# A causal linear attention in another order and a 64-tap convolution with one product a channel

## The reference, cut to what matters

```python
def _feat(x):
    return jax.nn.elu(x) + 1.0
def step(carry, xs):
    Si, Zi = carry
    q, k, v = xs
    Si = Si + jnp.einsum('bhd,bhk->bhdk', k, v)
    Zi = Zi + k
    num = jnp.einsum('bhd,bhkd->bhk', q, Si)
    Vi = num / (q * Zi + EPS_CAUSAL)
    return ((Si, Zi), Vi)
...
Q_lin = _feat(Q)
K_lin = _feat(Kp)
V_lin = _causal_linear_attn(Q_lin, K_lin, V)
return new_values @ Wo + bo
```

```python
K = jnp.einsum('md,ldk,dk->lk', C, A_powers, B)
...
conv_full = jnp.fft.irfft(Uf * Kf[None], n=n, axis=1)
start = (L - 1) // 2
y = conv_full[:, start:start + seq_len, :]
y = y + D[None, None, :] * u
```

## Time and profile before

| | before |
|---|---|
| median of 3 runs | 3556.96 us |
| profiled execution | 3555.08 us |
| its span | 3553.3 us |
| mean granted clock of PE | 0.911 |
| PE busy over the span | 2896.8 us (82%) |
| DVE busy over the span | 2011.3 us (57%) |
| first cross attention, from its first key update to its end | 998.2 to 1197.3 us |
| convolution stage | 2310.8 to 2402.6 us |

### The profile page before, as it was taken

How to read it: one execution, slowest core, us unless ns; L and a number is a source line. 1 busy time by engine, 2 the same in 40 slices (tenths; PEclk the granted TensorE clock), 3 DMA queues, 4 the chain that set the end, 5 groups by cost and what they waited for, 6 DMA issues and landing times. The chain is left out here.

```text
span 3553.3 us, 59085 instructions
## 1 busy us (share of the span) xinstructions
PE 2896.8 (82%) x21229; PEld 2114.5 (60%) x21229; DVE 2011.3 (57%) x5009; ACT 1663.1 (47%) x3692; POOL 543.8 (15%) x530
## 2 busy tenths in 40 slices
PE   6999999999777788588799764556899969997897
PEld 5777777776555567356566531445696545554685
DVE  6776677767566623678666668626211673444323
ACT  6666666765432222366577527213332335554221
POOL 2111101110122142100000000000210003333422
PEclk8999999999988799799899887787899989999799
DMA  3111111110100268300000000051695010000486
GB/s 125 45 36 37 37 51 44 38 37 28 50 3 1 90 216 302 106 1 2 24 11 8 28 0 0 0 99 61 237 343 210 24 52 26 25 24 23 151 278 208
DMA packets 143184, 273.73 MB, mean 77 GB/s; under 512 B 50576, under 2 KB 105104, under 8 KB 138032
## 3 DMA queue, kind: packets, MB, share of 16 engines
q1 hardware_dynamic: 126544, 237.66, 20.7%
q0 software_dynamic: 8688, 23.78, 1.8%
q10 hardware_dynamic: 7664, 8.51, 0.7%
HBM read 222.17 MB, written 47.74 MB: 76 GB/s over the span
## 5 line engine op out<-in xcount | busy, mean ns | idle before, releaser
L3005 ACT ACTIVATE L0a_ex<-bank,L0a_nb 128x128 f32<-128x128 f32 x512 | 145.7, 368 | 124.9 <-PE bank L2934 124.4
L1430 POOL TENSOR_TENSOR L3x_p<-L3x_p,L3x_rsum 128x512 f32<-128x512 f32 x128 | 130.7, 1041 | 413.6 <-DVE L3x_rsum L1501 413.6
L3271 DVE TENSOR_TENSOR L0a_ru<-bank,L0a_um 128x512 f32<-128x512 f32 x128 | 88.2, 689 | 176.5 <-PE bank L2926 162.0
L1483 DVE CUSTOM_DVE_ANT_0 L3x_s<-bank,L3x_bias 128x512 f32<-128x512 f32 x128 | 87.1, 682 | 177.4 <-PE bank L1259 177.4
L3262 DVE SCALAR_TENSOR_TENSOR L0a_xf<-L0a_xc,L0a_conv,L0a_xf 128x256 f32<-128x256 f32 x432 | 178.3, 481 | 9.5 <-ACT L0a_xf L3067 8.0
L3183 POOL TENSOR_TENSOR L0a_sum_sq<-L0a_sum_sq,L0a_sq 128x512 f32<-128x512 f32 x56 | 73.1, 1306 | 697.1 <-ACT L0a_sq L3102 697.1
L2848 PE MATMUL bank<-x_feat,L0a_wx 128*128 128x256 f32 x576 | 138.2, 391 | 4.1 <-ACT L0a_xc L3054 4.1
L2934 PE MATMUL bank<-L0a_ru,L0a_vm 128*128 128x512 f32 x256 | 136.6, 616 | 0.0
L2891 PE MATMUL bank<-x_feat,L0a_wz 128*128 128x256 f32 x512 | 118.4, 382 | 8.5 <-DVE L0a_yacc L3362 6.2
L1483 DVE CUSTOM_DVE_ANT_0 L1x_s<-bank,L1x_bias 128x256 f32<-128x256 f32 x256 | 92.9, 420 | 56.3 <-PE bank L1259 41.1
L2848 PEld LDWEIGHTS bank<-x_feat,L0a_wx 128*128 128x128 f32 x576 | 108.7, 195 | 25.4 <-issue 7.0
(11 more groups left out here) (707 smaller groups left out, 7615.4 us busy)
## 6 DMA issues: line engine op xcount, KB each, us to landing
L2f_wt<-in_L2f_w SPq DMA_DIRECT2D x23, 2180.0 KB, 9.7
L0f_wt<-in_L0f_w SPq DMA_DIRECT2D x39, 898.0 KB, 6.4
L3f_wt<-in_L3f_w SPq DMA_DIRECT2D x39, 768.0 KB, 5.4
L0a_wx<-in_L0a_wx SPq DMA_DIRECT2D x72, 256.0 KB, 3.1
L0a_wz<-in_L0a_wz SPq DMA_DIRECT2D x32, 512.0 KB, 4.1
L2a_band<-conv_taps SPq DMA_DIRECT2D x4, 2048.0 KB, 21.3
context_keys_values<-L2f_zeros ACTq DMA_DIRECT2D x32, 256.0 KB, 4.3
L0f_xs<-rows_by_expert SPq DMA_DIRECT2D x39, 128.5 KB, 3.4
```

Source lines behind the costliest of these rows:

```text
L1430: nc.gpsimd.tensor_tensor(p_, p_, rsum[g // n % 2][:, g % n, :].to_broadcast([P, NK]), ALU.mult).then_inc(sig("divided"), 1)
L1483: ins = vec.tensor_tensor_reduce(out=s[:, at:at + nk], in0=bank[:, at:at + nk], in1=bias[r % 2][:, e, :], scale=-scale, scalar=3e38, op0=A ...
L3005: last = a(ex[g % 3][:, j, b * P:(b + 1) * P], bank[:, at:at + P], ACT.Exp, bias=nb[r % 2][:, b, h:h + 1])
L3271: rv.empty(vec.tensor_tensor(ru[g % 2][:], bank[:].rearrange("p (j t) -> p j t", j=2), um[:].unsqueeze(1).to_broadcast([P, 2, T]), ALU.mult))
```

## The change

In the first cross attention the query projection of the next row moves from step 2 to step 1, its value projection from step 3 to step 2. DVE's bias add of the row before moves from after masks and reciprocal of step 2 to ahead of the masks. The tap sums move from step 1, two rows late, to step 3, one row late, after the masks and before the key update.

In the convolution the reversed tokens are written as two halves of a window (first and second), and each channel is one product: 64 columns of taps, 32 columns of tokens (2 halves of 16 tiles), 64 partitions of a bank, even channels in the lower 64 and odd ones in the upper. One constant matrix takes the place of two. The copies are five for a row, six rows on ACT and two on DVE, from a bank of its own for each row. A full bank is added to x_res with four additions.

```diff
@@ layer2_attn
-        moved = sb("moved", [P, B, TB + 1, D])
+        window = sb("window", [P, 2, NT, D])
+        first, second = window[:, 0], window[:, 1]
...
+        BY_DVE = (3, 6)
+        def take(eng, copy, r):
+            eng.wait_ge(sig("flipped"), r + 1)
+            bank = c.banks[r][:].rearrange("p (t d) -> p t d", t=TB)
+            ts = slice(TB * r, TB * r + TB)
+            copy(first[0:96, ts, :], bank[0:96])
+            copy(first[96:128, TB * r + 1, :], bank[96:128, 0])
+            copy(second[64:128, ts, :], bank[0:64])
+            copy(second[32:64, ts, :], bank[96:128])
+            return copy(second[0:32, TB * r, :], bank[64:96, 1])
...
-                    xs = c.x[:, :, q * PER_BANK:(q + 1) * PER_BANK]
-                    vec.tensor_tensor(xs, xs, c.banks[q][:].rearrange("p (d t) -> p t d", t=NT), ALU.add)
+                    xs = c.x[:, :, q * PAIRS * 2:(q + 1) * PAIRS * 2].rearrange("p t (j e) -> p e t j", e=2)
+                    for e in range(2):
+                        for half in range(2):
+                            taken = c.banks[q][e * L:(e + 1) * L, :].rearrange("p (j h t) -> p h t j", h=2, t=NT)
+                            own = xs[half * L:(half + 1) * L, e]
+                            vec.tensor_tensor(own, taken[:, half], own, ALU.add)
...
-                    for kind in range(2):
-                        for i in range(2):
-                            last = nc.tensor.matmul(flip_bank(n, kind, i)[:], flip[:, kind, :],
-                                                    xn[n % 2][:, 2 * i:2 * i + 2, :].rearrange("p t d -> p (t d)"), start=True, stop=True)
+                    for i in range(2):
+                        nc.tensor.matmul(c.banks[2 * n + i][:], flip[:], xn[n % 2][:, 2 * i:2 * i + 2, :].rearrange("p t d -> p (t d)"),
+                                         start=True, stop=True).then_inc(sig("flipped"), 1)
...
-                    for q, (window, half) in enumerate(quarters):
-                        taps = band[g][:, j, half * L // 2:(half + 1) * L // 2]
-                        last = nc.tensor.matmul(c.banks[d // PER_BANK][q * L // 2:(q + 1) * L // 2, at:at + NT], taps, window(d),
-                                                start=True, stop=True)
+                    n, e = divmod(d, 2)
+                    at = n % PAIRS * 2 * NT
+                    last = nc.tensor.matmul(c.banks[n // PAIRS][e * L:(e + 1) * L, at:at + 2 * NT], band[g][:, j, :],
+                                            window[:, :, :, d], start=True, stop=True)
@@ layer0_xattn, tensor
-                        if gi == 2 and r + 1 < ROWS:
+                        if gi == 1 and r + 1 < ROWS:
                             pe.wait_ge(sig("sliced"), 2 * (r + 2))
                             features(r + 1, a_ring, wq, xb)
+                        if gi == 2 and r + 1 < ROWS:
                             tokens(d_ring, wk, cb[(r + 1) % 2])
-                        if gi == 3 and r + 1 < ROWS:
                             features(r + 1, a_ring, wv, cb)
@@ layer0_xattn, vector
+                        if gi == 2 and r:
+                            add(r - 1)
                         if gi == 3 and r + 1 < ROWS:
                             raw_keys(r + 1)
                         masks(u)
...
-                        if gi == 1 and 2 <= r <= CHUNKS + 1:
-                            sum_taps(r - 2)
-                        if gi == 1 and r == CHUNKS + 2:
+                        if gi == 3 and 1 <= r <= CHUNKS:
+                            sum_taps(r - 1)
+                        if gi == 3 and r == CHUNKS + 1:
                             add_skip()
-                        if gi == 2 and r:
-                            add(r - 1)
```

More of the change, by code:

```diff
@@ L2013, in layer2_attn @@
     L, W = TAPS, D // TAP_GROUPS
-    PER_BANK = BLK // NT
-    tiles = c.xT[:].rearrange("p k n -> p (k n)").rearrange("p (t d) -> p t d", d=D)
+    PAIRS = BLK // (2 * NT)
     with ExitStack() as stack:
@@ L2018, in layer2_attn @@
         band = [sb(f"band{g}", [P, W, L]) for g in range(TAP_GROUPS)]
-        moved = sb("moved", [P, B, TB + 1, D])
+        window = sb("window", [P, 2, NT, D])
+        first, second = window[:, 0], window[:, 1]
         stats, mv, rstd, floor = sb("stats", [P, NT, 6]), sb("mv", [P, NT, 2]), sb("rstd", [P, NT, 2]), sb("floor", [P, 1])
         xn = [sb(f"xn{i}", [P, 4, D]) for i in range(2)]
[L2022 to L2025, removed]
+        flip = sb("flip", [P, P])
+        by_row = lambda a: a.rearrange("p (r t) d -> p r t d", t=TB)
+        BY_DVE = (3, 6)
[8 more added lines that the diff above has]
+            return copy(second[0:32, TB * r, :], bank[64:96, 1])
         sig = Signals(nc, "L2a")
@@ L2029, in _ @@
             def _(sp):
-                sp.dma_start(flip[:], c.dram["flips"]).then_inc(sig("flip"), 16)
+                sp.dma_start(flip[:], c.dram["flip"]).then_inc(sig("flip"), 16)
                 rows = c.tap_rows.tensor
@@ L2038, in _ @@
             def _(pool):
-                nc.gpsimd.memset(moved[high, :, 0, :], 0.0).then_inc(sig("edges"), 1)
-                nc.gpsimd.memset(moved[low, :, TB, :], 0.0).then_inc(sig("edges"), 1)
+                nc.gpsimd.memset(by_row(first)[96:128, :, 0, :], 0.0).then_inc(sig("edges"), 1)
+                nc.gpsimd.memset(by_row(second)[0:32, :, 1, :], 0.0).then_inc(sig("edges"), 1)
             @block.vector
@@ L2080, in root, with copy @@
                     a(rstd[:, ts, 1], rstd[:, ts, 0], ACT.Exp, scale=-0.5).then_inc(sig("rstd"), 1)
[L2082 to L2089, removed]
+                def copy(out, bank):
+                    return a(out, bank, ACT.Copy)
                 nc.scalar.preload_act_table_set("natural_log_exp_and_others")
@@ L2097, in _ @@
                         root(n + 1)
-                    take(n)
+                    for r in (2 * n, 2 * n + 1):
+                        if r not in BY_DVE:
+                            take(act, copy, r).then_inc(sig("windows_act"), 1)
             @block.tensor
@@ L2104, in _ @@
                     pe.wait_ge(sig("normed"), n + 1)
-                    if n >= 2:
-                        pe.wait_ge(sig("moved_act"), 6 * (n - 1))
-                    for kind in range(2):
-                        for i in range(2):
-                            last = nc.tensor.matmul(flip_bank(n, kind, i)[:], flip[:, kind, :],
-                                                    xn[n % 2][:, 2 * i:2 * i + 2, :].rearrange("p t d -> p (t d)"), start=True, stop=True)
[L2111 to L2117, removed]
+                    for i in range(2):
+                        nc.tensor.matmul(c.banks[2 * n + i][:], flip[:], xn[n % 2][:, 2 * i:2 * i + 2, :].rearrange("p t d -> p (t d)"),
+                                         start=True, stop=True).then_inc(sig("flipped"), 1)
+                pe.wait_ge(sig("windows_act"), B - len(BY_DVE))
+                pe.wait_ge(sig("windows_dve"), len(BY_DVE))
                 pe.wait_ge(sig("edges"), 2)
@@ L3521, in pack_attention @@
     a["L2a_a"], a["L2a_d"], a["L2a_ldt"] = i["L2_attn_A"], cols(i["L2_attn_D"]), cols(i["L2_attn_log_dt"])
-    anti, half = np.eye(P, dtype=np.float32)[::-1], np.eye(P // 2, dtype=np.float32)[::-1]
-    a["flips"] = np.stack([anti, np.kron(np.eye(2, dtype=np.float32), half)], 1)
+    a["flip"] = np.roll(np.eye(P, dtype=np.float32)[:, ::-1], -P // 4, 1)
     a["iota64"] = np.broadcast_to(np.arange(64, dtype=np.float32), (P, 64))
```

15 lines of the change are left out of this document (9 added, 6 removed).

## The result

The changed kernel takes 3469.31 us, the median of four runs (3464.62 to 3473.23), beside 3556.89 us (3548.32 to 3563.17) of the kernel before. The ratio is 0.9755, with a 95% interval of 0.973 to 0.9779. The forecast was 3476, with a range of 3458 to 3504. The profiled execution took 3471.38 us, 83.7 less than before, with a span of 3469.6. The first cross attention, measured from the start of its part to the start of the next, went from 234.3 to 186.9 us (47.4 less), the convolution from 93.2 to 54.9 (38.4 less). Together that is 85.8. The other ten parts add 2 us up. Their code is unchanged, and a part whose code is the same in all profiles differs by more than that: the feed-forward part behind the cross attention takes 274.6 to 282.0 us in the eleven profiles of this document.

The account below looks back on a forecast made before the run. The prediction took waits to bound the cross attention loop and instruction count the convolution. Savings of 38 and 43 us, 81 together, took the profiled 3555.1 to 3474; the median lies 1.9 above: 3476 us, range 3458 to 3504.

Parts of the forecast that it names:

- What bounds the loop: First cross attention: a loop of waits; DVE's late bias add holds wk (4.29 us in one row), and the next row hangs on wk.
- The row that was followed in full: First cross attention, row starting at 1151.67, full clock, no tap sums: 17.3 us to the next key update instead of 21.08.
- The loop's sum: First cross attention, seven rows: DVE's work 122.1 plus waits 14 makes 136.1 us, so 38.4 saved.
- The wait before the division: First cross attention: division waits for the weighing after the key update, 0.73 us at full clock, 1.99 at half; 2.0 taken.
- Tap sums, last row: First cross attention: moved tap sums add no wait; the last row changes by 0, at most 1.4 us either way.
- the pair: Convolution: one load of 64 columns and stream of 32, taken as 32 ns, from 16 at best to 80 at worst.
- the first three quarters: Convolution: three quarters of the channels, three blocks at 5.4 to 6.7 us, done at 2351 to 2355.
- about when the last band is there: Convolution: three quarters of the channels end about when the fourth band lands (2351.9); last product 3 to 7 us after landing.
- four or five gaps: Convolution, sign of being right: four or five gaps among the products; 16 gaps still would show it wrong.
- That the gaps do not go with instructions: Convolution, first rival: 16 channels still cost a gap, 19 us saved there, 3500 us in all; chance 0.07.
- The loop found another wait: First cross attention, second rival: another wait lets only 20 of the 38 us come, 3494 us; chance 0.10.
- The slower case: Convolution, rival: 64-column pairs run one after the other at half clock, 214 ns each, 44 us lost, 3563 us; chance 0.02.

## Why the prediction was right

*What bounds the loop.* Right. The reading of the earlier trace rows as one chain, add to wk to the next key update, held: with the add ahead of the masks the hold is gone, and without that edit it stays. The row that was followed in full, at full clock and without tap sums, was to take 17.3 us; the two such rows took 16.8 and 17.0.

*The loop's sum* was 7.4 us too large: 136.1 for seven rows, 128.7 measured. In four other runs with the same code it was 0.5 to 5.8 too large (130.3 to 135.6). Both of its terms were mis-sized. The wait before the division, taken as 2.0 us in each row (14), was 6.9 in all in the seven rows, whose mean clock was 0.96, and 4.1 us came as a wait of masks for scores, which had no term; with small rests 11.7. And DVE's own work, taken as 122.1, was 117.0. How much too large the terms were changes from run to run: in the run with nine wide products the same seven rows had a mean clock of 0.91, waits of 15.2 and 120.5 of DVE's work. Lines view after, DVE in the seven rows (busy, mean ns of one, idle before):

```profile
L2635 DVE TENSOR_TENSOR L0x_att<-bank,L0x_causal 128x384 f32<-128x384 f32 x112 | 54.4, 547 | 4.1 <-PE bank L2467 4.1
...
L2614 DVE TENSOR_SCALAR L0x_den<-L0x_den 128x512 f32<-128x512 f32 x7 | 4.6, 664 | 0.2
L2607 DVE TENSOR_TENSOR L0x_cT<-bank,L0x_den 128x256 f32<-128x256 f32 x12 | 4.5, 418 | 6.9 <-PE bank L2481 6.9
```

L2614, at 664 ns, took 1105 ns in the same seven rows before (there L2611): 3.1 us of the 5.1. Where it goes is told in the last section.

*Tap sums, last row.* Right: the tap sums' place costs nothing, and the last row went from 24.55 to 23.15, the 1.4 us allowed.

*Convolution.* That the gaps go with instructions was right. The rule that loads run beside products only where the row group differs (the Trainium skill, "TensorE: Matmul & The Clock Gate", section "Part 3: Packing small matmuls — row/col tiling") does not hold for these pairs, which have one row group: loads last up to 227 ns and products 294, and yet a pair takes 53.3. The term that was mis-sized is the pair, 32 ns forecast. It was doubled from the bursts of the earlier trace rows, which took the same at either clock, and so had no part for the clock; with 64 columns and a stream of 32 a pair took 36.8 ns at 1.00, near the forecast, and 53.3 at 0.50, the clock that the stage got. (The window that was worked out for the first three quarters, 2351 to 2355, starts from 2335 at both ends; from 2337 it would reach to 2357.) The step behind it, "about when the last band is there", failed: not the band but PE at half clock was last, and the last product came 9.2 us after it, not 3 to 7. That cost 4 to 5 us of the forecast 43 (38.4 came). The count of "four or five gaps" was wrong too, for the same reason: slow pairs hide the blocks. The first product came 24.1 us after the start of the stage, where 24.2 to 26.2 were worked out, and DVE's last bank took 1.73 us.

*Rivals.* That the gaps do not go with instructions fell with the products of 32 columns. The loop found another wait, the masks', but of 4.1 us only (2.4 before). The slower case, pairs one by one at 214 ns, did not come: two lie side by side in 107 ns at half clock.

The two misses, in these profiles 7 to 9 us more saved in the loop and 4 to 5 less in the convolution, cancel in part; that 3469 lies so near 3476 is partly luck.

## What to carry to other kernels

Where two uses of one bank follow each other, put the read that frees it first on its engine, before moving the product that waits: moving the product alone gained 7 us of 46 by the rows, 13 of 50 by the medians. Count instructions before columns in a run of tiny products: with few enough of them the blocks hide, and from there on only PE's own clock is left. After a forecast that hits, compare term by term; misses of opposite sign hide in a sum.

## What the runs showed of the hardware

*A busy PE is not always at full clock.* PE was busy for 27.51 of 27.51 us in the convolution and yet at half clock. It had stood at 1.00 from 2284.5 us, while the last products of 512 columns ran, and fell at 2287.9, in PE's wait before the first pair. With three more products of 512 columns in that wait it stayed at 1.00 and fell to 0.50 after 264 pairs; with six more between the channels it stayed there to the end. But small products can have the full clock. In the kernel before, the convolution's still smaller products, with gaps between the bursts, ran at 1.00 for 30 us (2368.5 to 2399); windows view, ten of them:

```profile
2380.00:2390.00 10.00, 4.96 (x310) 4.60 (x301) 0.69 (x1) 0.00 (x0) 0.00 (x0) 1.00 0.02 3
```

The products of 32 columns of taps, without wide ones beside them, came to 1.00 as well (2318.40 to 2325.90 above). Why the products of the changed kernel did not stays open.

*A DVE instruction waits out a POOL product.* Timeline before, one row, DVE and POOL:

```profile
1071.25 4.68 POOL L2570 TENSOR_TENSOR L0x_t_ex<-L0x_t_ex,L0x_t_cm 128x1024 f32<-128x1024 f32 x2
1073.86 2.35 DVE L2611 TENSOR_SCALAR L0x_den<-L0x_den 128x512 f32<-128x512 f32 x1
```

Alone L2611 takes 0.43 us. Here it starts just after the second of POOL's two products has, and ends at 1076.21, 0.3 us after it (1075.93). The same holds for all nine such instructions (TENSOR_SCALAR from SBUF to SBUF) that met a POOL instruction in the seven rows, five before and four after: each ends 0.3 us behind one, and six of them became longer than 1 us. DVE's masks, which read a bank, took no longer where they met one (0.55 us at most before, 0.56 without a meeting). How long the meetings are changes from run to run: L2611 or L2614 took 7.7 and 9.9 us in the seven rows of the old order, 4.6 to 7.1 in five runs of the new one, the longest single one 2.65. The Trainium skill ("SBUF — State Buffer", section "Who interferes with whom") has it: the two engines share a pair of ports, and whichever issues first keeps it for its whole instruction, while the other is blocked. The trace agrees; no experiment here took POOL away, so that the 3.1 us come from it is read, not tested, and they are not a steady gain of the new order.
